# Attention blocks of a two-layer convolutional transformer: the addition of two key tiles opens VectorE's group, and the folded maxima are transposed behind the first scores

## The chip, the cores and the metric

One core of one Trainium2 chip runs the whole program. The time is the device time of the program in microseconds (us), the median of three runs. The engines are TensorE (PE; its weight loads are PEld in the rows), VectorE (DVE), ScalarE (ACT), GpSimd (POOL) and SyncE (SP), which issues most transfers.

## The reference, cut to what matters

The input x is 2 x 512 x 48 x 48 in float32, so 2304 positions per image. Layer 0 normalizes groups of channels and projects to q, k and v. Layer 1 adds a position embedding and projects again. Both layers then do the same attention with 8 heads of 64 channels, and project its output back with a residual:

```python
scores = jnp.einsum('bhqd,bhkd->bhqk', q, k) * scale
attn = jax.nn.softmax(scores, axis=-1)
o = jnp.einsum('bhqk,bhkd->bhqd', attn, v)
```

The softmax is taken over all 2304 keys of a query, with its maximum subtracted before the exponential. Everything is float32.

## The kernel before, in words

Five stages follow each other: the normalization and the first projections, the attention of layer 0, the output projection of layer 0 with the projections of layer 1, the attention of layer 1, and the last output projection. The change lies in `attention_stage` (L514 to L927), which runs twice.

**The unit of work.** A block t is 384 queries (CH) of one pair of heads (128 channels, 2 heads e) of one image. There are 2 x 4 x 6 = 48 blocks (NB) in each attention. The 2304 keys of a block are 18 tiles of 128 keys, taken in KC = 6 groups c of three tiles k. Scores stand with the keys on the partitions and 384 queries along the row, for both heads: a tile is 128 x 768.

**The way of one block.** For each tile, TensorE writes the scores to PSUM banks 2k and 2k+1 (L683). ScalarE copies them to `prob` in SBUF (L753). VectorE takes a running maximum over the tiles, two chains `run[0]` and `run[1]` (L858), and at the end folds the two into `fold` (L864). The maximum over the 128 keys of a partition column is then found by transposing `fold` on TensorE, six transposes of 128 x 128 into the unused columns 384 to 511 of the score banks (`turn`, L649 to L654), reducing along the row on VectorE in three parts r (`reduce`, L839 to L845), and spreading the result to all partitions by six more transposes (`broadcast_max`, L656 to L662). ScalarE copies the spread maxima to `mx` (L761). VectorE and GpSimd subtract `mx` from `prob`, VectorE for the first 208 of each 384 queries and GpSimd for the others, after VectorE's part (`shift_part`, L586 to L589, both operands in SBUF). ScalarE takes the exponential in place, one instruction per head (L769). TensorE forms the weighted sum with v (`weigh`, L694), and the sum over keys with a matrix of ones (`add_keys`, L711). For that sum VectorE adds two of a group's three tiles beforehand (`pair_tiles`, L866 to L871, both operands in SBUF), so that TensorE sums two tiles in place of three. The sums of keys are later transposed (`turn_den`, L667), inverted, spread (`spread_den`, L673) and multiplied in (L903).

**The order of the work.** Each engine has a `body(t, par)` that goes through the six groups, written out by hand. In group c of block t an engine also does the later steps of groups that lie a fixed number of groups behind: `behind(t, par, c, lag)` gives them. `SHIFT_LAG` is 8, `EXP_LAG` 9, `PAIR_LAG` 10 and `PV_LAG` 11. The order within a group:

- TensorE (L715 to L737): the transposes of block t-1's fold if c is 0 (`TURN_AT`), the broadcast of its maxima if c is 1 (`BROADCAST_AT`), `turn_den` of t-3 if c is 3, `spread_den` if c is 4; then the scores of the three tiles; then `weigh` and `add_keys` of the group 11 behind.
- VectorE (L905 to L925): for each k, the reduction of block t-1 if c is 0, or small steps of the denominators, and then the maximum of tile 3c+k (tiles 0 and 1 of a block have none: tile 2 is compared with tile 0 from `prob`, and tile 3 with tile 1); `fold_slots` if c is 5; then `pair_tiles` of the group 10 behind; then the subtraction of the group 8 behind.
- ScalarE (L798 to L816): the three copies, in group 1 each followed by a copy of the spread maxima, then the two exponentials of the group 9 behind.
- GpSimd (L824 to L830): its part of the subtraction, group by group, as soon as `copied` and `dve_shifted` allow.

**The waits that matter here.** The transposes of a fold wait for `folded` (L650). They, and every other transpose into the score banks, wait for the copy of the third tile of the group before: `bank_free(t, c, 2)` (L635 to L641), and so the broadcast in group 1 waits for the copy of tile 2. The scores of tile k wait for the copy of the tile that had the same banks. A reduction waits for `turned`, and also for the scores of block t's tile r (L840 to L842). The copy of tile k in group 0 waits for reduction k (L749 to L750), since both read the same banks; tile 2's waits for its maximum as well. `pair_tiles` waits for the exponentials of its group and for the sums of keys two groups earlier, since `two_tiles` has two buffers. `add_keys` waits for `paired` (L706).

`blocks` (L591 to L598) runs four bodies written out, a loop over pairs of bodies, and three bodies for the end.

Of the kernel before, what the change touches and what calls it, by code (L numbers as in the profile page):

```python
# [26 lines left out]
GN_EPS = 1e-5  # L27
NORM_STEPS = 10
SHIFT_DVE = 208
SHIFT_LAG, EXP_LAG, PAIR_LAG, PV_LAG = 8, 9, 10, 11  # L30
TURN_AT, BROADCAST_AT = 0, 1
PV_COPY_AT, DEN_TURN_AT, DEN_SPREAD_AT, STORE_AT = 4, 3, 4, 4

# [480 lines left out]
def attention_stage(nc, name, psum, bufs, qk_d, v_d, att_d, next_loads):  # L514
# [6 lines left out]
    with ExitStack() as ctx:  # L521
        def sem(n):
            return ctx.enter_context(nc.semaphore(f"{name}_{n}"))
# [9 lines left out]
        scored = sem("scored")  # L533
# [18 lines left out]
        def slot(t, s):  # L552
            return KT * t + s + 1

        def scored_count(g):
            return 2 * KT + g
# [10 lines left out]
        def before(t, n):  # L567
            return isinstance(t, int) and t < n

        def live(t):  # L570
            return not isinstance(t, int) or 0 <= t < NB

        def last(t):
            return isinstance(t, int) and t == NB - 1
# [7 lines left out]
        def behind(t, par, c, lag):  # L582
            d = (lag - c + KC - 1) // KC
            return t - d, (par + d) % 2, c - lag + d * KC
# [46 lines left out]
        def _(pe):  # L631
# [3 lines left out]
            def bank_free(t, c, k):  # L635
                if c > 0 or not before(t, 1):
                    pe.wait_ge(copied, slot(t, 3 * (c - 1) + k) if live(t) else slot(NB - 1, KT - 1))
                if c == BROADCAST_AT + 1 and not before(t, 1) and live(t - 1):
                    pe.wait_ge(mx_ready, 3 * (t - 1) + k + 1)
                if c > BROADCAST_AT + 1 and not live(t) and live(t - 1):  # L640
                    pe.wait_ge(mx_ready, 3 * t)  # L641
# [7 lines left out]
            def turn(t):  # L649
                pe.wait_ge(folded, t + 1)  # L650
                for e in range(2):
                    for r in range(3):
                        mm = nc.tensor.transpose(psum[:, 2 * r + e, CH:512], fold[:, e, r * P:(r + 1) * P], ident)
                mm.then_inc(turned, 1)  # L654
# [60 lines left out]
            def body(t, par):  # L715
                for c in range(KC):
                    spare_free(t, c)
                    if c == TURN_AT and not before(t, 1) and live(t - 1):
                        bank_free(t, c, 2)
                        turn(t - 1)  # L720
                    if c == BROADCAST_AT and not before(t, 1) and live(t - 1):
                        bank_free(t, c, 2)
                        broadcast_max(t - 1)
                    if c == DEN_TURN_AT and not before(t, 3) and live(t - 3):
                        bank_free(t, c, 2)
                        turn_den(t - 3)
                    if c == DEN_SPREAD_AT and not before(t, 3) and live(t - 3):
                        bank_free(t, c, 2)
                        spread_den(t - 3)
                    if live(t):  # L730
                        for k in range(3):
                            bank_free(t, c, k)
                            scores(t, par, c, k)
                    tv, pv, cv = behind(t, par, c, PV_LAG)
                    if live(tv):
                        weigh(tv, pv, cv)
                        add_keys(tv, pv, cv)  # L737
# [99 lines left out]
        @block.vector  # L837
        def _(dve):
            def reduce(t, r):  # L839
                dve.wait_ge(turned, t + 1)  # L840
                if live(t + 1):
                    dve.wait_ge(scored, scored_count(slot(t + 1, 3 * TURN_AT + r)))  # L842
                if not before(t, 1):
                    dve.wait_ge(broadcast, t)
                nc.vector.tensor_reduce(mcol[:, :, r], s_banks(r)[:, :, CH:512], AX.X, ALU.max).then_inc(reduced, 1)  # L845

            def maximum(t, par, s):
                r = run[s % 2]
                dve.wait_ge(scored, scored_count(slot(t, s)))
                if s < 4:  # L850
                    dve.wait_ge(copied, slot(t, s - 2))
                    if not before(t, 1):
                        dve.wait_ge(folded, t)
                    other = prob[par][:, :, s - 2, :]
                else:
                    dve.wait_ge(maxed, maxed_count(t, s - 2))
                    other = r[:, :, :]
                nc.vector.tensor_tensor(r[:, :, :], s_banks(s % 3)[:, :, 0:CH], other, ALU.max).then_inc(maxed, 1)  # L858

            def fold_slots(t):  # L860
                dve.wait_ge(maxed, maxed_count(t, KT - 1))
                if not before(t, 1):
                    dve.wait_ge(turned, t)
                nc.vector.tensor_tensor(fold[:, :, :], run[0][:, :, :], run[1][:, :, :], ALU.max).then_inc(folded, 1)  # L864

            def pair_tiles(t, par, c):  # L866
                dve.wait_ge(exp_done, 2 * group(t, c))
                if c >= 2 or not before(t, 1):
                    dve.wait_ge(pv_done, pv_count(t, c - 2))
                nc.vector.tensor_tensor(two_tiles[c % 2][:, :, :], prob[par][:, :, 3 * c, :],  # L870
                                        prob[par][:, :, 3 * c + 1, :], ALU.add).then_inc(paired, 1)  # L871

            def shift(t, par, c):
                if c == 0:
                    dve.wait_ge(mx_ready, 3 * (t + 1))
                dve.wait_ge(copied, slot(t, 3 * c + 2))
                shift_part(nc.vector, par, c, 0, CH if last(t) else SHIFT_DVE).then_inc(dve_shifted, 1)

            def sum_den(t, k):
                parts = slice(0, 1) if k == 1 else slice(1, 3)  # L880
                dve.wait_ge(den_turned, t + 1)
                if live(t + 3):
                    dve.wait_ge(scored, scored_count(slot(t + 3, 3 * DEN_TURN_AT + k)))
                if not before(t, 1):
                    dve.wait_ge(inverted, t)
                groups = psum[:, 3:6, CH:512].rearrange("p r (e o i) -> p r e o i", e=2, o=2)[:, parts, :, :, 0]
                nc.vector.tensor_reduce(dsum[:, parts, :], groups, AX.X, ALU.add).then_inc(den_summed, 1)

            def invert(t):
                dve.wait_ge(den_summed, 2 * (t + 1))  # L890
                if not before(t, 1):
                    dve.wait_ge(widened, t)
                nc.vector.reciprocal(dcol[:, :, :], dsum[:, :, :]).then_inc(inverted, 1)

            def norm(t, par, r):
                q = slice(r * P, (r + 1) * P)
                dve.wait_ge(spread, t + 1)
                if live(t + 3):
                    dve.wait_ge(scored, scored_count(slot(t + 3, 3 * DEN_SPREAD_AT + r)))
                dve.wait_ge(pv_copied, t + 1)  # L900
                if not before(t, 2):
                    dve.wait_ge(stored[par], 16 * (t // 2))
                nc.vector.tensor_tensor(ob[par][:, q], psum[:, 2 * r, CH:512], pvr[:, q], ALU.mult).then_inc(normed, 1)  # L903

            def body(t, par):  # L905
                for c in range(KC):
                    for k in range(3):
                        if c == TURN_AT and not before(t, 1) and live(t - 1):
                            reduce(t - 1, k)
                        if c == DEN_TURN_AT and k > 0 and not before(t, 3) and live(t - 3):  # L910
                            sum_den(t - 3, k)
                            if k == 2:
                                invert(t - 3)
                        if c == DEN_SPREAD_AT and not before(t, 3) and live(t - 3):
                            norm(t - 3, 1 - par, k)
                        if 3 * c + k >= 2 and live(t):
                            maximum(t, par, 3 * c + k)
                    if c == KC - 1 and live(t):
                        fold_slots(t)
                    tp, pp, cp = behind(t, par, c, PAIR_LAG)  # L920
                    if live(tp) and not last(tp):
                        pair_tiles(tp, pp, cp)
                    ts, ps, cs = behind(t, par, c, SHIFT_LAG)
                    if live(ts):
                        shift(ts, ps, cs)  # L925

            blocks(dve, body)  # L927


# [167 lines left out]
```

## Time and profile before

| what | value |
|---|---|
| median of 3 runs | 4245.89 us (4245.76 to 4246.07) |
| profiled execution, its own time | 4246.06 us |
| span of the profile | 4244.3 us |
| TensorE (PE) busy | 4090.6 us, 96% |
| VectorE busy | 3200.4 us, 75% |
| ScalarE busy | 2775.9 us, 65% |
| GpSimd busy | 1408.4 us, 33% |
| mean granted TensorE clock | 0.992 |

The span goes from the first to the last instruction; about 2 us of the execution's time lie around it. Busy shares are means over five stages. The two attentions lie at about 430 to 1985 and 2520 to 4110 us. The page's slices show VectorE and ScalarE at eight to nine tenths there, and at three tenths or less in the projections. In a timeline a row is one instruction, or several alike that follow each other (xN): the start in us from the span's start, the duration, engine, line, operation, output and inputs with their shapes, and in brackets the idle time of the engine before it and what ended it.

### The profile page before, as it was taken

Reading aid. Unit: us, or ns where it says so; the run is one execution under the profiler, and the core shown is the slowest. Engines: PE = TensorE matmul, PEld = TensorE weight load, DVE = VectorE, ACT = ScalarE, POOL = GpSimd, SP = SyncE. Lnnn points to the kernel's source line nnn. Section 1 sums busy time; section 2 is a strip of 40 time slices with the busy share of each in tenths; the row PEclk is TensorE's granted clock in tenths of the full one; section 3 lists DMA queues with packets and bytes.
Section 4 is the critical chain, followed back from the end, with each engine's and each line's share of the span. In section 5 each row is a group of like instructions: output and inputs, shape, how many; then the busy total and the mean of one; then the engine's idle time right before and its main releaser. Section 6 shows DMA issues by size and latency. Waiting matters only on the chain. (4 is left out here: it accounts for less than half of the span.)

```text
span 4244.3 us, 88521 instructions
## 1 busy us (share of the span) xinstructions
PE 4090.6 (96%) x30024; PEld 1908.3 (45%) x30024; DVE 3200.4 (75%) x4032; ACT 2775.9 (65%) x3557; POOL 1408.4 (33%) x572
## 2 busy tenths in 40 slices
PE   7999899999999999998999989999999999999989
PEld 4554344444444444444555544444444444444445
DVE  3111899999999999997322239999999999999962
ACT  1112888888888888885000018888888888888840
POOL 0000344444444444443100004444444444444420
PEclk9999999999999999999999999999999999999999
DMA  4112000101000000011323220101000000000116
GB/s 175 74 74 93 10 27 19 37 13 32 20 28 22 22 24 24 26 49 53 117 100 126 97 95 9 30 19 33 19 28 24 22 22 26 24 20 30 41 45 215
DMA packets 157933, 208.42 MB, mean 49 GB/s; under 512 B 9008, under 2 KB 144304, under 8 KB 156848
## 3 DMA queue, kind: packets, MB, share of 16 engines
q1 hardware_dynamic: 137712, 179.28, 12.8%
q10 hardware_dynamic: 20160, 28.32, 1.8%
q8 instruction: 39, 0.64, 0.1%
q14 instruction: 22, 0.18, 0.0%
HBM read 113.19 MB, written 94.37 MB: 49 GB/s over the span
## 5 line engine op out<-in xcount | busy, mean ns | idle before, releaser
L589 POOL TENSOR_TENSOR prob<-prob,mx 128x1056 f32<-128x1056 f32 x564 | 1387.4, 2460 | 2627.5 <-DVE prob L589 2627.5
L753 ACT ACTIVATE prob<-psum_att 128x768 f32<-128x768 f32 x1728 | 1364.5, 822 | 951.7 <-PE psum_att L683 538.0
L683 PE MATMUL psum_att<-qst,kst 64*128 64x384 f32 x6912 | 1289.0, 505 | 30.6 <-DMA kst<-qk_scratch 18.0
L769 ACT ACTIVATE prob<-prob 128x1152 f32<-128x1152 f32 x1152 | 1291.2, 1172 | 17.3 <-POOL prob L589 15.1
L858 DVE TENSOR_TENSOR run<-psum_att,run 128x768 f32<-128x768 f32 x1344 | 1233.8, 950 | 36.1 <-PE psum_att L683 34.6
L694 PE MATMUL psum_att<-prob,vst 128*32 128x384 f32 x13824 | 1242.1, 491 | 0.7 <-ACT prob L769 0.5
L683 PEld LDWEIGHTS psum_att<-qst,kst 64*128 64x128 f32 x6912 | 623.6, 188 | 534.0 <-ACT prob L753 101.4
L589 DVE TENSOR_TENSOR prob<-prob,mx 128x1248 f32<-128x1248 f32 (+1 forms) x576 | 850.7, 1478 | 0.0
L694 PEld LDWEIGHTS psum_att<-prob,vst 128*32 128x32 f32 x13824 | 394.6, 109 | 755.3 <-issue 703.7
L870 DVE TENSOR_TENSOR two_tiles<-prob 128x768 f32<-128x768 f32 x564 | 565.3, 1002 | 1.1 <-ACT prob L769 1.1
L309 PE MATMUL psum<-xc_l,wq 128*128 128x384 f32 x1536 | 504.6, 490 | 9.3 <-DVE xc_l L382 4.4
L711 PE MATMUL psum_att<-prob,const_sb 128*32 128x384 f32 x2400 | 485.0, 486 | 0.0
L711 PE MATMUL psum_att<-two_tiles,const_sb 128*32 128x384 f32 x2256 | 463.6, 486 | 3.1 <-DVE two_tiles L870 3.1
L309 PEld LDWEIGHTS psum<-xc_l,wq 128*128 128x128 f32 x1536 | 294.0, 192 | 220.5 <-issue 20.8
L858 DVE TENSOR_TENSOR run<-psum_att,prob 128x768 f32<-128x768 f32 x192 | 183.7, 958 | 100.1 <-PE psum_att L683 100.1
L350 ACT ACTIVATE qk_l<-psum,par_sb 128x384 f32<-128x384 f32 x96 | 55.9, 582 | 308.7 <-PE psum L309 308.7
L424 DVE TENSOR_TENSOR vo_l<-psum,bv 128x512 f32<-128x512 f32 x36 | 24.9, 692 | 308.3 <-PE psum L326 308.3
L176 PE MATMUL psum<-attc_l,wo_l 128*128 128x384 f32 x768 | 254.1, 492 | 3.3 <-PEq L521 3.3
L711 PEld LDWEIGHTS psum_att<-two_tiles,const_sb 128*32 128x32 f32 x2256 | 139.0, 110 | 221.6 <-issue 216.4
L176 PEld LDWEIGHTS psum<-attc_l,wo_l 128*128 128x128 f32 x768 | 147.9, 193 | 106.9 <-issue 7.4
L406 DVE TENSOR_TENSOR qk_l<-psum,emb_table 128x384 f32<-128x384 f32 x96 | 53.3, 557 | 188.0 <-PE psum L309 188.0
L711 PEld LDWEIGHTS psum_att<-prob,const_sb 128*32 128x32 f32 x2400 | 146.8, 110 | 8.4 <-issue 7.5
(55 smaller groups left out, 1593.9 us busy)
## 6 DMA issues: line engine op xcount, KB each, us to landing
qk_scratch<-qk_l SPq DMA_DIRECT2D x48, 768.0 KB, 3.5
v_scratch<-vo_l SPq DMA_DIRECT2D x24, 768.0 KB, 3.5
qst<-qk_scratch SPq DMA_DIRECT2D x96, 192.0 KB, 2.4
kst<-qk_scratch SPq DMA_DIRECT2D x96, 192.0 KB, 2.4
vst<-v_scratch SPq DMA_DIRECT2D x96, 192.0 KB, 2.5
att_scratch<-ob ACTq DMA_DIRECT2D x96, 192.0 KB, 1.9
attc_l<-att_scratch SPq DMA_DIRECT2D x24, 768.0 KB, 5.7
x_sb<-in_x SPq DMA_DIRECT2D x8, 1152.0 KB, 14.0
```

What stands on the lines that cost most here:

```text
L176: mm = nc.tensor.matmul(bank, w[c], att[:, c, :], start=(c == 0), stop=(c == CT - 1))
L309: mm = nc.tensor.matmul(qk_bank(m), qkv["w"][:, c, m * P:(m + 1) * P], xc[p][:, c, :], start=(c == 0), stop=(c == CT - 1))
L350: nc.scalar.activation(qk[half][:, mt, :], qk_bank(m), ACT.Identity, bias=bias[:, m:m + 1])\
L406: nc.vector.tensor_tensor(qk[half][:, mt, :], qk_bank(m), emb_of(i, m), ALU.add)\
L589: return engine.tensor_tensor(x, x, m, ALU.subtract)
L683: mm = nc.tensor.matmul(psum[:, 2 * k + e, 0:CH], kst[rows, (3 * c + k) * P:(3 * c + k + 1) * P], qst[par][rows, :], start=True, stop=True ...
L694: mm = nc.tensor.matmul(psum[d:d + 32, 6, 0:CH], vst[:, kt, d:d + 32], prob[par][:, d // D, kt, :], start=(kt == 0), stop=(kt == KT - 1), ...
L711: mm = nc.tensor.matmul(psum[r:r + 32, 7, 0:CH], ones[:, :], tile, start=(c == 0 and n == 0), stop=(c == KC - 1 and (n == len(rounds) - 1 ...
L753: nc.scalar.activation(prob[par][:, :, s, :], s_banks(k)[:, :, 0:CH], ACT.Copy).then_inc(copied, 1)
L769: nc.scalar.activation(x, x, ACT.Exp, scale=SCALE).then_inc(exp_done, 1)
L858: nc.vector.tensor_tensor(r[:, :, :], s_banks(s % 3)[:, :, 0:CH], other, ALU.max).then_inc(maxed, 1)
L870: nc.vector.tensor_tensor(two_tiles[c % 2][:, :, :], prob[par][:, :, 3 * c, :], prob[par][:, :, 3 * c + 1, :], ALU.add).then_inc(paired, 1)
```

## The change

Two orders are changed. On VectorE the addition of two key tiles moves from near the end of a group, ahead of the subtraction, to the group's opening, and its lag goes from 10 to 11 groups: it is thus made one place later, behind the subtraction of the group before. On TensorE the six transposes of the folded maxima move from before the scores of group 0 to behind them, still before the weighted sum. The reductions no longer wait for scores, since the transposes are behind them.

```diff
-SHIFT_LAG, EXP_LAG, PAIR_LAG, PV_LAG = 8, 9, 10, 11
+SHIFT_LAG, EXP_LAG, PAIR_LAG, PV_LAG = 8, 9, 11, 11
@@ TensorE, body
                 for c in range(KC):
                     spare_free(t, c)
-                    if c == TURN_AT and not before(t, 1) and live(t - 1):
-                        bank_free(t, c, 2)
-                        turn(t - 1)
                     if c == BROADCAST_AT and not before(t, 1) and live(t - 1):
...
                         for k in range(3):
                             bank_free(t, c, k)
                             scores(t, par, c, k)
+                    if c == TURN_AT and not before(t, 1) and live(t - 1):
+                        bank_free(t, c, 2)
+                        turn(t - 1)
                     tv, pv, cv = behind(t, par, c, PV_LAG)
                     if live(tv):
                         weigh(tv, pv, cv)
@@ VectorE, reduce
                 dve.wait_ge(turned, t + 1)
-                if live(t + 1):
-                    dve.wait_ge(scored, scored_count(slot(t + 1, 3 * TURN_AT + r)))
                 if not before(t, 1):
                     dve.wait_ge(broadcast, t)
@@ VectorE, body
                 for c in range(KC):
+                    tp, pp, cp = behind(t, par, c, PAIR_LAG)
+                    if live(tp) and not last(tp):
+                        pair_tiles(tp, pp, cp)
                     for k in range(3):
...
                     if c == KC - 1 and live(t):
                         fold_slots(t)
-                    tp, pp, cp = behind(t, par, c, PAIR_LAG)
-                    if live(tp) and not last(tp):
-                        pair_tiles(tp, pp, cp)
                     ts, ps, cs = behind(t, par, c, SHIFT_LAG)
                     if live(ts):
                         shift(ts, ps, cs)
```

## Rows read from the trace of the kernel before

**Rows 1.** The page, busy us (share of the span) and instructions of each engine

```profile
PE 4090.6 (96%) x30024; PEld 1908.3 (45%) x30024; DVE 3200.4 (75%) x4032; ACT 2775.9 (65%) x3557; POOL 1408.4 (33%) x572
```

**Rows 2.** TensorE's waits: line, releaser, us in total, times, longest us

```profile
PE psum_att L653 <- DVE fold L864: 56.2, 92, 2.1
```

**Rows 3.** One block: length, each engine's busy us, granted clock, DMA share, GB/s

```profile
1010.81:1043.27 32.46, 31.79 (x282) 13.97 (x283) 30.82 (x39) 28.24 (x37) 14.75 (x6) 1.00 0.18 55
```

**Rows 4.** Timeline of TensorE around a boundary between blocks

```profile
1042.21 0.49 PE L711 MATMUL psum_att<-prob,const_sb 128*32 128x384 f32 x1
1043.27 0.84 PE L653 MATMUL psum_att<-const_sb,fold 128*128 128x128 f32 x6 [0.58 <-DVE fold L864]
1044.05 2.21 PE L683 MATMUL psum_att<-qst,kst 64*128 64x384 f32 x12
1046.18 2.14 PE L694 MATMUL psum_att<-prob,vst 128*32 128x384 f32 x24
...
1048.48 0.49 PE L711 MATMUL psum_att<-two_tiles,const_sb 128*32 128x384 f32 x1
...
1048.90 0.87 PE L660 MATMUL psum_att<-const_sb,mcol 128*128 128x128 f32 x6
```

**Rows 5.** Timeline of VectorE around the same boundary

```profile
1042.17 0.96 DVE L864 TENSOR_TENSOR fold<-run 128x768 f32<-128x768 f32 x1
...
1043.91 1.45 DVE L589 TENSOR_TENSOR prob<-prob,mx 128x1248 f32<-128x1248 f32 x1
1045.28 0.80 DVE L845 TENSOR_REDUCE mcol<-psum_att 128x2 f32<-128x256 f32 x2
1046.30 0.43 DVE L845 TENSOR_REDUCE mcol<-psum_att 128x2 f32<-128x256 f32 x1 [0.22 <-PE psum_att L683]
1046.67 0.96 DVE L858 TENSOR_TENSOR run<-psum_att,prob 128x768 f32<-128x768 f32 x1
1047.55 1.16 DVE L870 TENSOR_TENSOR two_tiles<-prob 128x768 f32<-128x768 f32 x1
```

**Rows 6.** Timeline of ScalarE around the same boundary

```profile
1040.89 2.22 ACT L753 ACTIVATE prob<-psum_att 128x768 f32<-128x768 f32 x3
...
1047.80 0.81 ACT L753 ACTIVATE prob<-psum_att 128x768 f32<-128x768 f32 x1 [0.46 <-DVE run L858]
```

**Rows 7.** Timelines, two handovers: ScalarE to TensorE, TensorE to VectorE

```profile
1031.58 0.81 ACT L753 ACTIVATE prob<-psum_att 128x768 f32<-128x768 f32 x1
...
1032.44 0.55 PE L673 MATMUL psum_att<-const_sb,dwide 128*128 128x128 f32 x3
...
4098.56 0.55 PE L667 MATMUL psum_att<-const_sb,den 128*128 128x128 f32 x3
...
4099.14 0.24 DVE L887 TENSOR_REDUCE dsum<-psum_att 128x2 f32<-128x4 f32 x2 [5.42 <-PE psum_att L667]
```

**Rows 8.** Timelines of VectorE and GpSimd in the second layer's tail

```profile
4064.07 1.08 DVE L845 TENSOR_REDUCE mcol<-psum_att 128x2 f32<-128x256 f32 x3
...
4067.47 1.45 DVE L589 TENSOR_TENSOR prob<-prob,mx 128x1248 f32<-128x1248 f32 x1
4069.08 3.25 DVE L870 TENSOR_TENSOR two_tiles<-prob 128x768 f32<-128x768 f32 x1 [0.17 <-ACT prob L769]
...
4069.06 2.46 POOL L589 TENSOR_TENSOR prob<-prob,mx 128x1056 f32<-128x1056 f32 x1 [2.32 <-DVE prob L589]
```

**Rows 9.** Timeline of GpSimd at the boundary of rows 4

```profile
1045.44 2.45 POOL L589 TENSOR_TENSOR prob<-prob,mx 128x1056 f32<-128x1056 f32 x1 [3.34 <-DVE prob L589]
```

**Rows 10.** Timelines of VectorE and GpSimd in the first layer's tail

```profile
1962.30 1.44 DVE L589 TENSOR_TENSOR prob<-prob,mx 128x1248 f32<-128x1248 f32 x1
1963.91 0.96 DVE L870 TENSOR_TENSOR two_tiles<-prob 128x768 f32<-128x768 f32 x1 [0.16 <-ACT prob L769]
...
1964.24 2.94 POOL L589 TENSOR_TENSOR prob<-prob,mx 128x1056 f32<-128x1056 f32 x1 [2.67 <-DVE prob L589]
```

**Rows 11.** Timeline of TensorE at the second block of layer 1

```profile
2540.71 0.98 PE L653 MATMUL psum_att<-const_sb,fold 128*128 128x128 f32 x6 [2.15 <-DVE fold L864]
```

## The prediction, made before the changed kernel ran

> **What bounds the kernel now.** I read the page's line of engines first, then TensorE's waits, then one period of the attention, engine by engine. The page has TensorE busy for 96% of the span [rows 1], so only what TensorE executes or waits for can move the time much. Its waits have one entry that recurs with every block of queries: 92 waits, 56.2 us, of the transposes of the folded maxima (L653) for VectorE's fold (L864) [rows 2]. The attention repeats with 32.46 us per block, at a granted clock of 1.00, VectorE busy 30.82 us of it and ScalarE 28.24 us [rows 3]. So TensorE leads, and VectorE is close behind it; both have to be followed.
>
> One boundary between blocks, on TensorE [rows 4]: the last matmul of the sums of keys starts at 1042.21, the transposes at 1043.27, the scores of group 0 at 1044.05, the weighted sum at 1046.18, the broadcast at 1048.90. From the last matmul of a group to whatever follows, TensorE otherwise takes 0.42 us (1048.48 to the broadcast, which waits for nothing); here it takes 1.06. The fold costs **0.64 us** per block. VectorE ends the fold at 1043.13 [rows 5], so TensorE follows it in 0.14.
>
> **Part 1, the transposes behind the scores of group 0.** Nothing is added or removed on TensorE: six transposes and twelve score matmuls change places. Unchanged spacings: 0.42 from the sums to what follows; 0.78 from the first transpose to what follows; 2.13 from the first score matmul to what follows [rows 4]. The one spacing without a row is scores to transposes. Bounds: the step from one score matmul to the next is about 0.15 (12 in 2.21 with the last near 0.5), the whole last matmul 0.5; from its start to the weighted sum it is 0.42, inside the 2.13. I take 0.42, the nearest row; the ends are -0.27 and +0.1 us per block. Thus the scores start at 1042.63, the transposes at 1044.76 and the weighted sum at 1045.54, against 1046.18: 0.64 won. The fold (1043.13) is then 1.6 us early. The scores' own cover: the banks must have been copied, and the last copy of the previous block ends at 1043.11 [rows 6] while the third tile's scores start about 1.24 after the first, at 1043.87. Covered by 0.7.
>
> What comes late next is the **reduction**. Before, the transposes were done before the scores, so the three reductions ran as each tile's scores ended: the third started at 1046.30, 0.12 after the weighted sum's start, then maximum at 1046.67, copy of tile 2 on ScalarE at 1047.80 to 1048.61 [rows 5, 6]. Broadcast waits for that copy (bank_free at c = 1); it had 0.29 us to spare, and so none of it showed. Now the reductions can't start until all six transposes end. From the first transpose's start T: 0.87 for six [rows 4], 0.03 to VectorE (transposes of the denominators end at 4099.11, the reduction starts at 4099.14 [rows 7]); first to third reduction 0.65 (three in 1.08 with 0.43 each, [rows 8]); third reduction to end of the copy 2.31 [rows 5, 6]; copy to TensorE 0.05 (1032.39 to 1032.44 [rows 7]). That is T + 3.91. TensorE's own work reaches the broadcast at T + 0.78 + 2.72 = T + 3.50. So a **new wait of 0.41 us** appears at L660. Bounds: 0.3 if the transposes' modelled end is late by a tenth; 0.75 if reductions go at their full 0.43 and the handover takes the 0.17 that VectorE to ScalarE takes (1047.63 to 1047.80). Behind the waiting broadcast stand the scores of group 1, and with them VectorE's maxima, which follow at their old distance. VectorE itself is free for the reduction 2.66 after the first scores, if the addition stands ahead of it (below), and the transposes end at 3.03: covered by 0.37.
>
> **Part 2, the addition first in the group, lag 11.** No instruction more or fewer; each group's addition (0.95) and subtraction (1.45) change places, and the addition is now made just before the maxima of the same group whose sums of keys use it. TensorE reads it after scores and weighted sum, 4 us after the group starts, so 2 us and more remain. Its exponentials ended a group earlier, as before: cost nothing. The subtraction comes 0.87 earlier, which alone would let GpSimd start earlier. But the addition then starts 1.37 us after the subtraction (the spacing from it to the next instruction on VectorE, 1043.91 to 1045.28 [rows 5]), and GpSimd starts its part 1.53 after it (1045.44 [rows 9]). They overlap, and that is where the trace has a warning. At the first layer's end an addition at 1963.91 came 1.61 after its subtraction and ran its plain 0.96; GpSimd started late, at 1964.24, and ended 2.31 after the addition [rows 10]. At the second layer's end the addition started 0.02 behind GpSimd and took 3.25 us, ending 0.81 after GpSimd had [rows 8]. Whoever is first makes the other wait. In steady state the addition leads by 0.16, so GpSimd waits: it ends 1.37 + 0.95 + 2.31 = 4.63 after the subtraction began, while the next subtraction comes 0.87 + 0.87 + 2.6 = 4.8 to 4.9 after it. Hidden; in group 0 it is a tie, as now (1.16 us for an addition instead of 0.95 [rows 5]). The subtraction's reader, the exponentials, stand behind copy 2. I take 0 for the whole part.
>
> The Trainium skill (SBUF — State Buffer, "Who interferes with whom") says that a VectorE instruction with two SBUF inputs and a GpSimd instruction that reads SBUF exclude each other, and that the order of issue decides who blocks. The two stretches above agree; the rule does not say who is first here, and speaks against this change if GpSimd is.
>
> **The ends of the layers.** The second block of a layer waits 2.15 us for its fold [rows 11]; its reductions now follow at once, about 2 us won per layer. Of the 96 transposes of folds four wait for nothing (92 waits in the list); they pay the 0.41. In each layer's tail the cycle of subtraction and held-up addition is 4.8 us (1.61 + 3.25, less 0.07 of overlap [rows 8]); with the addition first it is 1.37 + 0.95 + 2.31 less 0.1, about 4.5: an estimate of 1.7 us per layer.
>
> **Sum.** Of the 92 waits two are at the starts and two in the tails, where no scores cover the fold and nothing changes. 88 x (0.64 - 0.41) = 20.2; starts 2 x 2.0 = 4.0; the four -1.6; tails 3.4. Together 26.0 us: 4246.06 - 26.0 = 4220. The profiled execution took 4246.06 us (span 4244.3), 0.17 above the median of the runs, so nothing is to be converted.
>
> **Rivals.** A difference of 0.2% is 8.5 us, about what a measurement of this kernel can tell from none.
> (a) *The new wait eats the gain.* With 0.61 to 0.80 at L660, between my value and the upper bounds of both steps, the result is 4238 to 4255, about 4243. For: the bounds allow it, and the chain has four handovers. Against: each piece but one has its row. Chance 0.14, and 0.05 that the same goes past 0.2% slower.
> (b) *No new wait.* If the reductions and the copy kept pace, 88 x 0.64 + 7.4 = 64 us, 4182. Against: the chain would have to be 0.4 shorter than its rows. Chance 0.08.
> (c) *GpSimd is first*, slower. The place is the start of VectorE's group, the price 3.25 - 0.95 = 2.3 us of VectorE per addition; it decides if an addition reaches VectorE later than 1.53 after the subtraction, by a wait or a jump. In every group: VectorE needs 30.82 + 6 x 2.3 = 44.6 us a block, 12.2 more than the period, 92 x 12.2 = 1122, so 5370. In group 0 alone: reductions 2.0 later, wait 2.4 at L660, 88 x 1.75 = 154, so 4400. Against: the margin of 0.16, and both semaphores long reached. Chance 0.07.
> That the edit does nothing at all is excluded: the fold's wait is recorded and the scores do not depend on it.
>
> **The numbers.** Forecast 0.66, its own range 4205 to 4237 (new wait 0.25 to 0.6); (a) 0.14 same and 0.05 slower, (b) 0.08, (c) 0.07. Faster 0.74, same 0.14, slower 0.12. The range reaches down to the forecast's low end and up through (a) to 4250; (b), (c) and the rest of (a) stay out.
>
> **What the changed profile should show.** No L653 wait for L864 except at the end of each layer; L660 waiting for L753 some 0.4 us in nearly every block; a period of 32.2; an addition 1.37 after each subtraction at 0.95 us, GpSimd's instruction later or longer by about 0.4 to 0.9. Wrong if additions take 3 us, if L660's wait is above 0.6, or if the spacing from scores to transposes differs from 2.13.

## The result, and the profile after

The changed kernel takes 4263.82 us (median of 6 runs, 4262.62 to 4265.45) against 4246.02 us before (6 runs, 4245.76 to 4247.35): a ratio of 1.0042, 95% interval 1.0029 to 1.0055. It is **slower by 17.8 us**, where 26 us less were forecast, and outside the range. The span of its profile is 4260.9 us, 16.6 more than before. Among the runs of the kernel before that belong to the second group of experiments below, one took 7981 us at a granted clock of 0.881; it is left out of every ratio.

From the page of the changed kernel, the engines' line (as [rows 1]) and one group of instructions: line, engine, operation, output and inputs, busy us and mean ns, then the idle time of TensorE before it and what ended it.

```profile
PE 4086.6 (96%) x30024; PEld 1905.1 (45%) x30024; DVE 3180.3 (75%) x4032; ACT 2774.5 (65%) x3557; POOL 1771.1 (42%) x572
...
L660 PE MATMUL psum_att<-const_sb,mcol 128*128 128x128 f32 x576 | 84.4, 283 | 81.4 <-ACT prob L753 81.4
```

GpSimd is busy for 1771 us where it was 1408; TensorE executes the same work. The fold's wait of [rows 2] is gone but for the layers' tails, and the broadcast has one of 81.4 us. From the view of all waits (engine, line, releaser, us in total, times, longest):

```profile
PE psum_att L660 <- ACT prob L753: 81.4, 94, 3.3
...
DVE mcol L843 <- PE psum_att L653: 36.8, 93, 1.7
DVE run L856 <- ACT prob L753: 26.3, 88, 0.3
```

The first row is the new wait, 94 times, 0.87 us each on average: more in total than the 56.2 us that it replaces. In the steady blocks the idle time is 0.77 and 0.87 us in turn; the longest, 3.3 us, stands at the start of the second layer. The second row says that the reductions now start when the transposes end, as forecast. The **third row was not forecast**: VectorE's maximum waits 88 times, 0.3 us each, for a copy by ScalarE.

The same boundary between blocks as in [rows 4], in the timeline of TensorE of the changed kernel:

```profile
1012.19 0.49 PE L711 MATMUL psum_att<-prob,const_sb 128*32 128x384 f32 x1
1012.61 2.21 PE L683 MATMUL psum_att<-qst,kst 64*128 64x384 f32 x12
1014.74 0.88 PE L653 MATMUL psum_att<-const_sb,fold 128*128 128x128 f32 x6
1015.55 2.14 PE L694 MATMUL psum_att<-prob,vst 128*32 128x384 f32 x24
...
1019.10 0.86 PE L660 MATMUL psum_att<-const_sb,mcol 128*128 128x128 f32 x6 [0.77 <-ACT prob L753]
```

The scores follow the sums of keys after 0.42 us, so the 0.64 us of the fold are won; the transposes come 2.13 behind the first scores, as put; the weighted sum 0.81 behind them. TensorE could then have started the broadcast 2.72 later, at 1018.27. It starts at 1019.10: **0.83 us** of wait, against a forecast of 0.41.

VectorE, in answer to [rows 5]:

```profile
1012.19 0.96 DVE L862 TENSOR_TENSOR fold<-run 128x768 f32<-128x768 f32 x1
1013.07 1.45 DVE L589 TENSOR_TENSOR prob<-prob,mx 128x1248 f32<-128x1248 f32 x1
1014.43 0.95 DVE L868 TENSOR_TENSOR two_tiles<-prob 128x768 f32<-128x768 f32 x1
1015.66 1.09 DVE L843 TENSOR_REDUCE mcol<-psum_att 128x2 f32<-128x256 f32 x3 [0.27 <-PE psum_att L653]
1017.03 0.96 DVE L856 TENSOR_TENSOR run<-psum_att,prob 128x768 f32<-128x768 f32 x1 [0.29 <-ACT prob L753]
1017.91 1.45 DVE L589 TENSOR_TENSOR prob<-prob,mx 128x1248 f32<-128x1248 f32 x1
```

VectorE does the fold, the subtraction and the addition, and could go on at 1015.30 (0.87 after the addition began), before the transposes end at 1015.62. The three reductions take 1.09 together, 0.33 from one to the next, as forecast. But the maximum of tile 2 starts 1.37 after the first reduction, not the 1.02 of the forecast (0.65 to the third reduction and 0.37 from there to the maximum). ScalarE's copies (in answer to [rows 6]) and GpSimd (to [rows 9]) say why:

```profile
1016.19 1.51 ACT L753 ACTIVATE prob<-psum_att 128x768 f32<-128x768 f32 x2 [0.96 <-DVE mcol L843]
1018.16 0.81 ACT L753 ACTIVATE prob<-psum_att 128x768 f32<-128x768 f32 x1 [0.45 <-DVE run L856]
...
1014.60 3.11 POOL L589 TENSOR_TENSOR prob<-prob,mx 128x1056 f32<-128x1056 f32 x1 [2.68 <-DVE prob L589]
```

The copy of tile 0 starts 0.53 after the first reduction and ends 0.81 later, at 1017.00; the maximum compares tile 2 with that copy, and starts at 1017.03. The copy of tile 2 then ends at 1018.97. In the kernel before, at the boundary of [rows 5], the copies of tiles 0 and 1 have this row:

```profile
1045.83 1.51 ACT L753 ACTIVATE prob<-psum_att 128x768 f32<-128x768 f32 x2 [0.61 <-DVE mcol L845]
```

There the copy of tile 0 starts 0.55 after the first reduction and ends at 1046.64; the maximum starts at 1046.67.

In the changed kernel GpSimd starts 1.53 after the start of VectorE's subtraction and its instruction is 3.11 long: it ends 4.64 after the subtraction began, where 4.63 was put.

Every second block is a little worse. In the next boundary of the same timelines, TensorE and then VectorE:

```profile
1047.41 0.87 PE L653 MATMUL psum_att<-const_sb,fold 128*128 128x128 f32 x6
...
1051.88 0.86 PE L660 MATMUL psum_att<-const_sb,mcol 128*128 128x128 f32 x6 [0.87 <-ACT prob L753]
...
1048.41 1.09 DVE L843 TENSOR_REDUCE mcol<-psum_att 128x2 f32<-128x256 f32 x3 [0.40 <-PE psum_att L653]
```

From the transposes to the first reduction it is 1.00 us here and 0.92 in the boundary above, and from the transposes to the broadcast 4.47 and 4.36. The blocks of the first layer alternate between 32.63 and 32.82 us (spacing of VectorE's folds). The loop also goes over pairs of blocks, but that its jump is the reason was not tried and is not shown. Before, the steady blocks took 32.46.

### The profile page after: what moved, and what is told of

Same layout as the page of the kernel before. It is cut to its first block and busy times, and to the rows that moved or that the text cites. A ratio compares the mean times of both kernels' runs of the same rounds, so it can differ in the third digit from the quotient of the medians.

```text
span 4260.9 us, 88251 instructions
## 1 busy us (share of the span) xinstructions
PE 4086.6 (96%) x30024; PEld 1905.1 (45%) x30024; DVE 3180.3 (75%) x4032; ACT 2774.5 (65%) x3557; POOL 1771.1 (42%) x572
## 5 line engine op out<-in xcount | busy, mean ns | idle before, releaser
L589 POOL TENSOR_TENSOR prob<-prob,mx 128x1056 f32<-128x1056 f32 x564 | 1750.1, 3103 | 2282.4 <-DVE prob L589 2282.4
L868 DVE TENSOR_TENSOR two_tiles<-prob 128x768 f32<-128x768 f32 x564 | 536.9, 952 | 0.0
L660 PE MATMUL psum_att<-const_sb,mcol 128*128 128x128 f32 x576 | 84.4, 283 | 81.4 <-ACT prob L753 81.4
```

The costliest lines, as they stand in the source:

```text
L589: return engine.tensor_tensor(x, x, m, ALU.subtract)
L660: mm = nc.tensor.transpose(psum[:, 2 * r + e, CH:512], mcol[:, e, r:r + 1].broadcast_to([P, P]), ident)
```

## The experiments

All ratios are against runs of the kernel before on the same chip, made together with those of the experiment. "Period" is the mean spacing of VectorE's folds between 900 and 1500 us in the profile. The experiments were run in three groups, each with its own runs of the kernel before: 4245.8 us in the first (rows three to six of the table), 4245.4 in the second (the next four), 4242.3 in the third (the last three). Where a text below compares an experiment with the changed kernel (4263.8), the two come from different groups, and differences of less than 4 us between groups mean nothing.

| run | us | ratio, 95% interval | period |
|---|---|---|---|
| before | 4246.0 | 1 | 32.46 |
| changed | 4263.8 | 1.0042 (1.0029 to 1.0055) | 32.73 |
| transposes only | 4266.2 | 1.0050 (1.0037 to 1.0064) | 32.72 |
| addition only | 4242.8 | 0.9994 (0.9985 to 1.0003) | 32.46 |
| changed, no wait for tile 0 | 4225.5 | 0.9952 (0.9937 to 0.9967) | 32.33 |
| changed, reductions early | 4225.9 | 0.9953 (0.9938 to 0.9969) | 32.34 |
| transposes behind first tile | 4223.4 | 0.9948 (0.9931 to 0.9966) | 32.28 |
| changed, broadcast by tile | 4215.7 | 0.9931 (0.9913 to 0.9949) | 32.23 |
| both by tile | 4167.4 | 0.9822 (0.9804 to 0.9839) | 31.72 |
| both by tile, old addition | 4171.9 | 0.9825 (0.9807 to 0.9843) | 31.68 |
| before, broadcast and spreading by tile | 4226.1 | 0.9963 (0.9949 to 0.9977) | 32.30 |
| changed, broadcast and spreading by tile | 4199.6 | 0.9900 (0.9883 to 0.9916) | 32.06 |
| GpSimd first | 5023.3 | one run | 40.97 |

### The two parts of the change, each alone

The transposes alone: the changed kernel with the addition put back.

```diff
-SHIFT_LAG, EXP_LAG, PAIR_LAG, PV_LAG = 8, 9, 11, 11
+SHIFT_LAG, EXP_LAG, PAIR_LAG, PV_LAG = 8, 9, 10, 11
@@ VectorE, body: pair_tiles from the group's opening back to behind fold_slots
```

> Only the transposes of the fold move behind the scores of group 0; the addition keeps lag 10 and its old place. Theory A (the late reductions, and behind them tile 0's copy on ScalarE, hold up the broadcast): the whole loss comes with this part, 4262 to 4266 us, wait of L660 for L753 about 0.8 us a block, period 32.7. Theory B (the addition behind the subtraction and GpSimd's longer instructions cost the time): most of the loss goes away, and 4220 to 4240 us are seen, since the fold's wait is gone and the port is left as it was.

TensorE's waits in that run:

```profile
PE psum_att L660 <- ACT prob L753: 81.4, 94, 3.3
```

The addition alone: the kernel before, with `pair_tiles` at the opening and lag 11.

> Only the addition moves to the group's opening with lag 11; the transposes stay ahead of the scores. Theory A: 4246 us within 4, period 32.46, the fold's wait of 0.64 as before, GpSimd's instructions 3.1 us in place of 2.45 and nobody waiting for them. Theory B: 4262 us or more.

TensorE's waits there:

```profile
PE psum_att L653 <- DVE fold L864: 56.4, 92, 2.1
```

The loss comes whole with the transposes (4266.2), and the wait at L660 is the same 81.4 us to the tenth. The addition alone leaves the period and the fold's wait as they were, and is not slower: 3 us less, with an interval that includes no change. GpSimd is busy for 1770 us in it, so the 360 us that GpSimd's instructions grew by cost nothing. Theory B is ruled out.

### What makes the new wait twice as long as forecast

The maximum without the wait for tile 0 (tile 0 is left out of the maximum):

```diff
-                if s < 4:
+                if s == 2 and not before(t, 1):
+                    dve.wait_ge(folded, t)
+                    other = fold[:, :, :]
+                elif s < 4:
                     dve.wait_ge(copied, slot(t, s - 2))
```

> The changed kernel, but the first maximum of a block compares tile 2 with the fold of the block before in place of tile 0 of its own, so tile 0 is left out of the maximum and the wait for ScalarE's copy of tile 0 is gone. Theory A: the maximum follows the third reduction in 0.37 us in place of 0.6 to 0.7, the wait at L660 falls from 0.83 to about 0.5, and the time by 90 x 0.33 = 30 us to 4234. Rival (only the reductions matter, the copy of tile 0 is hidden): 4264 us, wait 0.83.

TensorE's transposes, VectorE's reductions and maximum, and TensorE's broadcast behind them:

```profile
1007.97 0.88 PE L653 MATMUL psum_att<-const_sb,fold 128*128 128x128 f32 x6
...
1008.88 1.09 DVE L843 TENSOR_REDUCE mcol<-psum_att 128x2 f32<-128x256 f32 x3 [0.30 <-PE psum_att L653]
1009.89 0.95 DVE L859 TENSOR_TENSOR run<-psum_att,fold 128x768 f32<-128x768 f32 x1
...
1011.95 0.87 PE L660 MATMUL psum_att<-const_sb,mcol 128*128 128x128 f32 x6 [0.38 <-ACT prob L753]
```

The maximum now starts 1.01 after the first reduction and the wait on TensorE falls from 0.77 to 0.38. From the transposes to the broadcast it is 3.98 us, where it was 4.36. The time falls by 38 us, more than the 30 expected, to 4225.5, which lies inside the forecast's range. So the copy of tile 0 was on the path, and cost more than the forecast's whole gain.

The first reduction earlier, all else as changed:

```diff
-                for e in range(2):
-                    for r in range(3):
+                for r in range(3):
+                    for e in range(2):
                         mm = nc.tensor.transpose(psum[:, 2 * r + e, CH:512], fold[:, e, r * P:(r + 1) * P], ident)
-                mm.then_inc(turned, 1)
+                    mm.then_inc(turned, 1)
@@ reduce
-                dve.wait_ge(turned, t + 1)
+                dve.wait_ge(turned, 3 * t + r + 1)
@@ fold_slots
-                    dve.wait_ge(turned, t)
+                    dve.wait_ge(turned, 3 * t)
```

> The changed kernel with the six transposes ordered by reduction, and a signal after every second one in place of one after the sixth, so the first reduction may start about 0.45 us earlier. Theory A: VectorE is free only 2.69 us after the first scores (end of the addition), against 3.05 now, so the reductions come 0.36 earlier, the wait at L660 falls to about 0.47 and the time by 32 us to 4232. Rival (TensorE's order alone costs the time): 4264 us.

```profile
1008.43 0.95 DVE L868 TENSOR_TENSOR two_tiles<-prob 128x768 f32<-128x768 f32 x1
1009.30 1.08 DVE L843 TENSOR_REDUCE mcol<-psum_att 128x2 f32<-128x256 f32 x3
1010.67 0.96 DVE L856 TENSOR_TENSOR run<-psum_att,prob 128x768 f32<-128x768 f32 x1 [0.29 <-ACT prob L753]
...
1012.74 0.86 PE L660 MATMUL psum_att<-const_sb,mcol 128*128 128x128 f32 x6 [0.41 <-ACT prob L753]
```

The reductions follow the addition after 0.87 us, with no idle time: VectorE's own work is what they wait for now. The maximum still waits 0.29 for the copy of tile 0, and the wait on TensorE is 0.41. 38 us are won against 32 expected. Both runs say the same of the chain: what starts it earlier or shortens it comes back almost one to one in each of some 90 blocks (the periods fall by 0.40 and 0.39 us).

### Another place for the transposes

The kernel before, with the transposes behind the scores of the first tile alone:

```diff
@@ TensorE, body: turn(t - 1) no longer ahead of the scores
...
                         for k in range(3):
                             bank_free(t, c, k)
                             scores(t, par, c, k)
+                            if k == 0 and c == TURN_AT and not before(t, 1) and live(t - 1):
+                                bank_free(t, c, 2)
+                                turn(t - 1)
```

> The kernel before with the transposes of the fold behind the scores of the first tile of group 0, so two tiles are scored after them. Theory A: the fold is done in time, the reductions start when VectorE is free, 2.66 us after the first scores as before, TensorE pays 0.27 us for one more change between scores and transposes, and about 0.2 us of wait at L660 appears: 0.64 - 0.27 - 0.2 = 0.17 won per block, 4230 us. Rival (transposes behind any scores cost the time): 4260 us or more.

TensorE at the boundary:

```profile
1004.53 0.92 PE L683 MATMUL psum_att<-qst,kst 64*128 64x384 f32 x4
1005.38 0.87 PE L653 MATMUL psum_att<-const_sb,fold 128*128 128x128 f32 x6
1006.19 1.56 PE L683 MATMUL psum_att<-qst,kst 64*128 64x384 f32 x8
1007.68 2.14 PE L694 MATMUL psum_att<-prob,vst 128*32 128x384 f32 x24
...
1010.64 0.86 PE L660 MATMUL psum_att<-const_sb,mcol 128*128 128x128 f32 x6 [0.18 <-ACT prob L756]
```

Four score matmuls, six transposes, eight score matmuls: 3.15 us from the first scores to the weighted sum, where the changed kernel takes 2.94 (1012.61 to 1015.55). The additional turn costs 0.21, not 0.27. The wait at L660 is 0.18. The result, 4223.4 us, is 22 below before (16 were expected), and 40 below the changed kernel. Transposes behind scores are thus no loss in themselves; behind *all* the scores they are late for what VectorE and ScalarE make of them.

### Not waiting for all tiles at once

The broadcast's six transposes go by tile, each pair waiting only for the copy that frees its own banks:

```diff
-                        bank_free(t, c, 2)
                         broadcast_max(t - 1)
@@ broadcast_max
-                for e in range(2):
-                    for r in range(3):
+                for r in range(3):
+                    bank_free(t + 1, BROADCAST_AT, r)
+                    for e in range(2):
```

> The changed kernel, but the six transposes of the broadcast go by tile and each pair waits only for the copy of the tile whose banks it writes, where all six waited for tile 2's. Theory A: four of the six run before tile 2's copy is done, the wait shrinks from 0.83 by four steps of 0.12 to about 0.35, and the time by 43 us to 4221. Rival (the wait is passed on whole, since the last pair still needs tile 2's copy and the scores of group 1 stand behind it): 4258 to 4264 us.

```profile
1005.37 0.88 PE L653 MATMUL psum_att<-const_sb,fold 128*128 128x128 f32 x6
...
1008.90 1.19 PE L661 MATMUL psum_att<-const_sb,mcol 128*128 128x128 f32 x6
```

The broadcast's six start 0.81 + 2.72 after the fold's, without a wait, and take 1.19 in place of 0.87: 0.32 us of the wait are left, inside them. 48 us are won (43 expected).

With `spread_den` changed in the same way in group 4, and the fold's transposes still with one signal:

> The changed kernel with broadcast and spreading by tile, but the fold's transposes still with one signal after all six. Theory A: 0.16 us a block below the run with the broadcast by tile alone, 4201 us, with about 0.3 us left in the middle of the broadcast; the rest down to the best run is the earlier first reduction.

```profile
1039.13 0.65 PE L661 MATMUL psum_att<-const_sb,mcol 128*128 128x128 f32 x4
1040.00 0.43 PE L661 MATMUL psum_att<-const_sb,mcol 128*128 128x128 f32 x2 [0.21 <-ACT prob L753]
```

Here the gap shows as a row of its own: four transposes, 0.21 of idle time for ScalarE's copy, two more. 4199.6 us, near the 4201 expected. The stretch from the denominators' transposes to the spreading falls from 5.48 us in the changed kernel (1029.61 to 1035.09) to 5.33 (1050.07 to 1055.40).

All three together, signals by tile as well:

> Fold transposes by tile with a signal each, broadcast by tile, and the spreading of the denominators in group 4 by tile in the same way. Theory A: no wait is left at L660, the 0.15 us at L673 goes too, the period falls to about 31.75 us (TensorE's own work) and the time to 4180 us. Rival: another wait takes their place, VectorE being busy 30.65 us of a period, and 4200 us or more are seen.

TensorE's two sets of transposes, then VectorE:

```profile
1027.76 0.87 PE L653 MATMUL psum_att<-const_sb,fold 128*128 128x128 f32 x6
...
1031.28 0.87 PE L661 MATMUL psum_att<-const_sb,mcol 128*128 128x128 f32 x6
...
1028.28 1.08 DVE L843 TENSOR_REDUCE mcol<-psum_att 128x2 f32<-128x256 f32 x3
1029.67 0.96 DVE L856 TENSOR_TENSOR run<-psum_att,prob 128x768 f32<-128x768 f32 x1 [0.31 <-ACT prob L753]
```

From the fold's transposes to the broadcast it is 3.52, and 0.87 for the six: **no wait is left** there in the steady blocks. The maximum of tile 2 still waits 0.31 for the copy of tile 0, but TensorE no longer waits for what follows from it. The time is 4167.4 us, 1.8% below before; 4180 was expected, from a period of 31.75 (measured 31.72), so most of the difference lies outside the steady blocks.

> As e7, but with the addition at its old place and lag 10. Theory A: the place of the addition only matters in the layers' tails, so 2 to 5 us above e7, with the same period. Rival (the new place frees VectorE for the reductions or holds it up): the periods differ by 0.1 us or more.

4171.9 us: 4.6 above, and the period is not longer (31.68). The intervals of the two runs overlap, so it is not shown that the addition's place is worth anything here; if it is, then not in the steady blocks.

> The kernel before, order untouched, with the broadcast and the spreading by tile. Theory A: the broadcast waited for nothing there and the fold's wait stays; only the 0.16 us at L673 goes, 92 times: 4231 us. Rival (going by tile gains by itself, whatever the order): 4200 us or less.

4226.1 us, 16 below before (15 expected): the order of the kernel before gains only the spreading's 0.16, since its broadcast had no wait to lose. Between this run and "both by tile, old addition", which leaves the addition where it was, the period falls from 32.30 to 31.68, by 0.62 us of the fold's 0.64. The two differ in the place of the transposes and in the signal after every second of them; that signal with the old order alone was not run. So the transposes behind the scores gain about what was forecast for TensorE **once** the chain behind them is short enough.

### GpSimd first

The changed kernel with `pair_tiles` called after k = 0 in each group, so behind the first maximum:

> The changed kernel with the addition one place later in each group, behind the first maximum (or first reduction), so that GpSimd's subtraction has begun before it. If whoever begins first holds the other off until its end, the additions take 2.5 us in place of 0.95 and GpSimd's instruction 2.45 in place of 3.1; VectorE then needs 30.65 + 6 x 1.6 = 40 us a block and becomes the bound: about 4950 us (4800 to 5000). If the two share the port instead, both grow by some tenths and the time stays under 4300 us.

The engines' line of its page, and the group of the additions among VectorE's lines:

```profile
PE 4321.7 (86%) x30024; PEld 1911.6 (38%) x30024; DVE 3644.5 (73%) x4032; ACT 2835.1 (56%) x3557; POOL 1405.8 (28%) x572
...
L868 DVE TENSOR_TENSOR two_tiles<-prob 128x768 f32<-128x768 f32 x564 | 1007.7, 1787 | 0.0
```

One group and the addition of the next, in the timeline of VectorE, then of GpSimd:

```profile
1003.99 1.45 DVE L589 TENSOR_TENSOR prob<-prob,mx 128x1248 f32<-128x1248 f32 x1
1005.36 0.95 DVE L856 TENSOR_TENSOR run<-psum_att,run 128x768 f32<-128x768 f32 x1
1006.22 2.58 DVE L868 TENSOR_TENSOR two_tiles<-prob 128x768 f32<-128x768 f32 x1
...
1013.83 1.40 DVE L868 TENSOR_TENSOR two_tiles<-prob 128x768 f32<-128x768 f32 x1
...
1005.52 2.47 POOL L589 TENSOR_TENSOR prob<-prob,mx 128x1056 f32<-128x1056 f32 x1 [4.14 <-DVE prob L589]
1011.98 2.44 POOL L589 TENSOR_TENSOR prob<-prob,mx 128x1056 f32<-128x1056 f32 x1 [3.99 <-DVE prob L589]
```

GpSimd begins at 1005.52 and takes its plain 2.47. The addition begins at 1006.22, 0.70 into it, and takes 2.58; it ends at 1008.80, 0.81 after GpSimd's end at 1007.99. The addition of the next group begins 1.85 into GpSimd's instruction, takes 1.40, and again ends 0.81 after it. The mean over all additions is 1787 ns where it was 952 in the changed kernel. The time is 5023.3 us in one run, 760 more than the changed kernel, from one place in an order.

The rival of this run, that the two share, is ruled out. Of the number, 4950 expected and 5023 measured, a part is luck. The 40 us a block (measured 40.97) were worked out from six additions of 2.5 us and a VectorE without idle time. In the block from 1003.99 three additions take 2.56 to 2.64 us and three take 0.95 to 1.40, by how far GpSimd has come, and over two blocks (1003.99 to 1085.90) VectorE is busy for 72.0 of 81.9 us. So VectorE's own work is not the bound by itself: the later maxima hold up ScalarE's copies, TensorE waits for these at three places in each block (1.73 us at L660, 1.72 at L667, 1.41 at L673 in this one), and VectorE in turn waits for TensorE's scores. The mean granted clock in this run is 0.968 against 0.994; what that costs was not separated.

## Why the prediction was wrong

The forecast was faster, the result slower. It is rival (a), "the new wait eats the gain", in its part beyond 0.2% slower, which had a chance of 0.05: the wait is 0.83 and 0.94 us in turn where 0.41 was put and 0.80 was rival (a)'s upper end. The prediction's own sign of being wrong, a wait above 0.6 at L660, is what the profile shows.

1. **The 0.64 us of the fold**: right. They are gone in the changed kernel (0.42 from sums to scores), and the fold waits only in the tails.
2. **Scores to transposes at 2.13**: right, 2.13. What follows the transposes comes 0.81 later, not 0.78: 0.03 us a block that the sum didn't have.
3. **The reductions start with the transposes' end** (T + 0.90): right in one block (0.92), 1.00 in the next.
4. **"Third reduction to end of the copy 2.31"**: this step failed. It was read from [rows 5, 6] as one stretch, with the maximum following the third reduction. The maximum has two conditions, and the second is the copy of tile 0, which in its turn waits for the *first* reduction. In the kernel before that copy ends at 1046.64 (its row stands with the result), and the maximum of [rows 5] starts at 1046.67, 1.39 after the first reduction (0.55 + 0.81 + 0.03). From the third reduction alone it could have started at about 1046.65 (0.35 later, the distance in the run without the wait). So the two conditions were already met within 0.02 us of each other, with no idle time in the row to show it. Before, the first reduction ran a full 1.02 ahead of the third, since the scores spread them. Now the third starts 0.66 after the first, and the hidden condition decides: 1.37 in place of 1.02, 0.35 us more. The run without it has 0.38 us of TensorE's wait back (3.98 in place of 4.36).
5. **"Copy to TensorE 0.05"**: 0.13 (1018.97 to 1019.10), 0.08 more. With the 0.35, and 0.02 from step 3, less the 0.03 by which TensorE itself comes later (step 2), that is 0.42 more than 0.41: the 0.83 of this boundary. In the next boundary the same steps give 0.94 (0.10, 0.38 and 0.09 more than put), so 0.89 on average.
6. **The sum**: 0.64 - 0.89 - 0.03 = -0.28 a block; the period grew by 0.27 (32.73 - 32.46). Times 90: 24 us lost. The span grew by 16.6 only, so 7 to 8 us came back at the ends of the layers. The two parts alone divide them: the addition alone has a span of 4239.8 with an unchanged period, 4.5 below before (3.4 put for the tails); the transposes alone a span of 4264.4, so 20.1 with 23.4 from the period, 3 us back at the starts (4.0 put, less the 1.6). These are spans of single profiles from different groups of runs, so they bear out the sizes only roughly.
7. **The addition costs nothing**: right, and for the reason given. It leads GpSimd by 0.17 us (0.16 put), keeps its 0.95, GpSimd's instruction grows by 0.66 and ends when it was said to. One sum of this part is written wrongly: the distance to the next subtraction, "0.87 + 0.87 + 2.6 = 4.8 to 4.9", needs 1.37 for its first term (the terms as written give 4.3). The value itself holds, 4.84 from 1013.07 to 1017.91, so GpSimd ends 0.20 before it. Rival (c) was a real one: its price per addition in the run with GpSimd first is 2.58 - 0.95 = 1.6 us where the addition comes 0.7 late; right behind GpSimd's start it was 2.3 in the tail of [rows 8].

The Trainium skill (SBUF — State Buffer, "Who interferes with whom") gives the rule that the two exclude each other and that the order decides; the 3.11 us of GpSimd in the changed kernel and the 2.58 us of the addition in the run with GpSimd first are the two sides of it.

The bound of 0.75 to 0.80 was built from longer handovers and slower reductions. It left out a path through another engine, and no widening of the known steps would have covered that except by chance. With that path taken away, the remaining errors (the handover and the transposes' 0.03) leave the result inside the range.

## What to carry to other kernels

When a step is moved so that several things which ran staggered now start together, don't carry over a duration that was read as one stretch: list for each instruction in it *every* semaphore it waits for, and work out when each would be reached. An instruction without idle time before it says nothing on its second-latest condition; here that was 0.02 us away. And when a move gives a wait that is as long as the one it took away, look at what the wait asks for: transposes in six different banks that wait for the last of three copies, or signal once at the end, can wait and signal by tile, and here that turned a loss of 18 us into a gain of 78. About 16 of the 78 come from the spreading of the denominators, which gains them in the old order too.

## What the runs showed of the hardware

- GpSimd held off by VectorE is shown as a longer instruction (3.11 us for 2.45), starting as long after the subtraction as before (1.53 us). In the page this looks like more work on GpSimd (1408 to 1771 us) for the same instructions, and is waiting.
- VectorE behind GpSimd ends 0.81 us after it in the tail [rows 8] and in the run with GpSimd first, whether it began 0.02, 0.70 or 1.85 us into GpSimd's instruction. So an addition of 0.95 us has nearly all of its length still before it when GpSimd has ended.
- One more change from score matmuls to transposes and back costs TensorE 0.21 us (3.15 us in the run with the transposes behind the first tile, 2.94 in the changed kernel, for the same eighteen instructions).
- The steady blocks of the kernel before took 32.45 to 32.47 us in the first layer. In the changed kernel even and odd blocks differ by 0.19 us, in the run with the transposes behind the first tile, where the fold's wait is gone as well, by 0.02 only. What makes the difference stays open.
